# Preparing a mixture-of-experts stage inside the last attention quad, and naming tile rows on GpSimd

## What is computed

```
x2 = rmsnorm(hid, ln2_w).reshape(-1, h)          # 2048 tokens
probs = softmax(x2 @ gate_w.T)                   # 16 experts
top_w, top_i = top_k(probs, 4); top_w /= sum(top_w)
act = silu(g) * u                                # g, u = x2 @ w1[e], 176 each
routed = einsum('te,teh->th', wfull, act @ w2)   # 4 experts of each token
shared = (silu(x2 @ sg.T) * (x2 @ su.T)) @ sh_down_w.T   # 352 wide, every token
out = hid + routed + shared
```

## Time and profile before

| | us |
|---|---|
| median of three runs (lowest, highest) | 1864.67 (1861.90, 1866.82) |
| the profiled execution | 1865.75 |
| its span | 1864.0 |
| PE busy | 1721.0 (92%) |
| DVE busy | 1156.7 (62%) |
| ACT busy | 983.2 (53%) |
| POOL busy | 500.3 (27%) |

### The profile page before, as it was taken

The page is one execution under the profiler, slowest core; times in us unless marked ns, Lnnn a source line. Parts: engine busy times, 40 slices in busy tenths (PEclk is TensorE's granted clock), DMA queues, the critical chain, the costliest instruction groups (busy, mean ns, idle before and its releaser), DMA issues. The chain is left out here.

```text
span 1864.0 us, 34272 instructions
## 1 busy us (share of the span) xinstructions
PE 1721.0 (92%) x11713; PEld 1450.5 (78%) x11722; DVE 1156.7 (62%) x2562; ACT 983.2 (53%) x2535; POOL 500.3 (27%) x554
## 2 busy tenths in 40 slices
PE   7999996897699999999999999999999967879997
PEld 6666663655588888888888888888888866679985
DVE  6689883897655656656556655555555546754444
ACT  2588875586344545444555545444444433445553
POOL 4133321253311111111112111111111110257773
PEclk7799996998899999999999999999999985989999
DMA  4111121302100100100100101000000015243347
GB/s 151 59 37 36 37 81 36 110 8 94 49 13 1 46 12 12 36 12 12 35 24 23 46 1 35 13 12 24 12 12 1 1 37 148 75 127 114 125 145 235
DMA packets 48916, 97.39 MB, mean 52 GB/s; under 512 B 7467, under 2 KB 29147, under 8 KB 47765
## 3 DMA queue, kind: packets, MB, share of 16 engines
q1 hardware_dynamic: 40023, 72.44, 12.8%
q0 software_dynamic: 7584, 21.37, 3.9%
q10 hardware_dynamic: 1144, 1.40, 0.2%
HBM read 73.85 MB, written 20.97 MB: 51 GB/s over the span
## 5 line engine op out<-in xcount | busy, mean ns | idle before, releaser
L1939 POOL TENSOR_TENSOR hold_wq<-hold_wq,ca_rsum 128x512 f32<-128x512 f32 x128 | 133.4, 1043 | 826.8 <-DVE ca_rsum L2167 826.8
L1835 ACT ACTIVATE hold_wq<-hold_wq,ca_nb,ca_evens 128x128 f32<-128x128 f32 x256 | 123.4, 484 | 242.4 <-DVE ca_nb L2162 242.4
L1835 ACT ACTIVATE hold_wq<-hold_wq,ca_nb,c_rqs 128x128 f32<-128x128 f32 x256 | 123.4, 483 | 225.5 <-DVE ca_nb L2162 225.5
L712 DVE TENSOR_REDUCE a_mx<-a_s 128x2 f32<-128x512 f32 x256 | 164.8, 681 | 41.8 <-PE a_s L584 39.1
L503 ACT ACTIVATE a_prob<-a_s 128x512 f32<-128x512 f32 x256 | 146.8, 605 | 59.2 <-PE a_s L604 58.0
L1949 PE MATMUL ca_qk<-c_xTh,ca_wqkv_h 128*128 128x512 f32 x384 | 161.5, 420 | 11.3 <-DVE ca_wqkv_l L2112 11.3
L1951 PE MATMUL ca_qk<-c_xTh,ca_wqkv_l 128*128 128x512 f32 x384 | 152.3, 397 | 0.0
L1950 PE MATMUL ca_qk<-c_xTl,ca_wqkv_h 128*128 128x512 f32 x384 | 151.6, 395 | 0.0
L2064 PE MATMUL ca_acc<-ca_wo_h,ca_oT_h 128*128 128x256 f32 x512 | 145.4, 284 | 0.0
L2066 PE MATMUL ca_acc<-ca_wo_h,ca_oT_l 128*128 128x256 f32 x512 | 144.6, 282 | 0.0
L2065 PE MATMUL ca_acc<-ca_wo_l,ca_oT_h 128*128 128x256 f32 x512 | 144.5, 282 | 0.0
(11 more groups left out here) (428 smaller groups left out, 4853.3 us busy)
## 6 DMA issues: line engine op xcount, KB each, us to landing
w_all<-slot_results SPq DMA_DIRECT2D x16, 512.0 KB, 7.4
mw_raw<-in_d_expert_w SPq DMA_DIRECT2D x16, 352.0 KB, 4.3
a_heads<-a_osb SPq DMA_DIRECT2D x124, 32.0 KB
a_wraw<-a_heads SPq DMA_DIRECT2D x31, 128.0 KB, 2.1
mw_down<-in_d_expert_d SPq DMA_DIRECT2D x1, 2816.0 KB
token_rows<-mw_rows SPq DMA_DIRECT2D x1, 2176.0 KB
hold_wk<-in_c_wkT SPq DMA_DIRECT2D x1, 2064.0 KB, 8.2
hold_wq<-in_c_wqT SPq DMA_DIRECT2D x1, 2064.0 KB
```

The lines of the kernel that those rows point to most:

```text
L712: dve.tensor_reduce(mx[:, b % 2, :, h], s1_bank(b, u)[:, :, :], AX.X, ALU.max)\
L1835: ins = act.activation(prob[:, p, b, :], prob[:, p, b, :], ACT.Exp, bias=nb[:, p, b:b + 1], scale=row_scale[layer][:, r:r + 1], accum_out= ...
L1939: pool.tensor_tensor(prob[:, k % 2, :, :], prob[:, k % 2, :, :], rsum[:, k % 2, :].unsqueeze(2).broadcast_to([P, GB, TOKENS]), ALU.mult)\
```

## The change

Three things are changed, and the rest follows from them.

1. A class `EarlyExpertData` lays tiles at fixed addresses over buffers that the last attention quad no longer uses. The transposed x of the attention and that of the experts are one tile (`own_T`, `early.x`). While the second layer starts, SP loads the shared gate and value weights, the gate's, the norm's and experts 14, 15 and 6. In the last quad, by tables like those of before: DVE's statistics of groups 0 to 2 (`gauge`, behind units 7, 11, 15), POOL's roots (`root`), DVE's normalisation (`shrink`, units 9, 13 and the end), PE's turns of pairs 0 to 3 (`FLIP`, units 10, 11, 14, 15), high and low halves of the weights (ACT, POOL; units 6, 7, 8, 9, 12). The sort stage keeps group 3's rows, `raw_d`, and 13 experts.
2. `named` is made by POOL from `tile_of` itself, comparison and multiplication in one operation, 64 of 128x80, for 16 on DVE and 64 on ACT. It waits for `placed`. Finding starts three units later.
3. POOL, which waits for nothing then, makes the low halves of nine experts, six ahead of the naming, three behind it. `down` no longer has a place free from the start, and is loaded in two parts at the end of the sort stage, behind all expert loads. X_EARLY is 14 for 22, X_AHEAD 26 for 28.

```diff
@@ attend_tokens
+        GAUGE = {7: 0, 11: 1, 15: 2}
+        ROOT = {8: 0, 12: 1}
+        SHRINK = {9: 0, 13: 1}
+        FLIP = {10: 0, 11: 1, 14: 2, 15: 3}
+        HALVE = {6: 0, 7: 1}
+        PARTS = {8: 0, 9: 1, 12: 2}
...
+                sp.wait_ge(x_lo, PAIRS)
+                sp.dma_start(early.raw_gu[:, :], early.gu_w).then_inc(ld_s, 16)
+                for n in range(len(EARLY_EXPERTS)):
+                    sp.dma_start(early.raw_w[n][:, :], early.expert_w[EARLY_EXPERTS[n]]).then_inc(ld_s, 16)
...
+                        if end in FLIP:
+                            turn(PAIRS + FLIP[end], rows, min(v_count(WHOLE - 1, 0, end + 1), UNITS * WHOLE))
...
-X_EARLY, X_AHEAD, X_BUFS = 22, 28, 40
+X_EARLY, X_AHEAD, X_BUFS = 14, 26, 40
+LATER_EXPERTS = (0, 1, 2, 3, 4, 5, 7, 8, 9, 10, 11, 12, 13)
+LOWERED = 9
...
@@ sort_and_share
             def _(sp):
...
-                sp.dma_start(first.down[:, :], first.w2).then_inc(first.ld_d, 16)
                 sp.wait_ge(meta_ready, 1)
-                sp.wait_ge(xn_ready, BATCHES)
+                sp.wait_ge(xn_ready, GB)
...
-                for n in range(RAW_BUFS, EXPERTS):
+                for n in range(RAW_BUFS, len(LATER_EXPERTS)):
                     sp.wait_ge(first.w_lo, n - RAW_BUFS + 1)
                     first.load(sp, n)
+                sp.wait_ge(u_psum, UNITS_S)
+                sp.dma_start(first.down[:, 0:LAST_DOWN], first.w2[:, 0:LAST_DOWN]).then_inc(first.ld_d, 16)
+                sp.wait_ge(acc_psum, UNITS_S)
+                sp.wait_ge(hid_lo, UNITS_S)
+                sp.wait_ge(d_lo, 1)
+                sp.dma_start(first.down[:, LAST_DOWN:], first.w2[:, LAST_DOWN:]).then_inc(first.ld_d, 16)
...
+                for n in range(6):
+                    first.split_lo(pool, early, n)
+                pool.wait_ge(ld_c, 32)
+                pool.wait_ge(placed, 1)
+                for b in range(BATCHES):
+                    after(pool, found_psum, b - DEEP + 1)
+                    for k in range(TOPK):
+                        c = P + b + BATCHES * k
+                        ins = pool.tensor_scalar(named[:, b % DEEP, k, :], times, tile_of[:, b, k:k + 1], cons[:, c:c + 1],
+                                                 ALU.is_equal, ALU.mult)
+                    ins.then_inc(named_ready, 1)
+                for n in range(6, LOWERED):
+                    first.split_lo(pool, early, n)
...
-                for m in range(PAIRS + 1):
-                    if m < PAIRS:
-                        turn(m)
-                    if m >= 1:
-                        score(m - 1)
-                for t in range(UNITS_S + 2):
+                for m in range(4):
+                    score(m)
+                turn(0)
+                turn(1)
+                gates_and_values(0)
+                turn(2)
+                turn(3)
+                for m in TURNS:
+                    score(m)
+                for t in range(1, UNITS_S + 2):
...
@@ routed_experts, down(0)
-                        pe.wait_ge(first.ld_d, 16)
+                        pe.wait_ge(first.ld_d, 32)
```

More of the change, by code:

```diff
@@ L1300, with pair_of, prepare_text_free @@
 UNITS = GROUPS * 4
[L1303 removed]
+def pair_of(rows, m, n):
+    return rows[:, m // 2, n, :, 2 * P * (m % 2):2 * P * (m % 2) + 2 * P]
+def prepare_text_free(nc, work, x_sb, ident, xn, ctx_sb, own_T, image_T, rqs, nrqs, ob, g, loads, fetch):
     with ExitStack() as stack:
@@ L1613, in fetch, with attend_tokens @@
         self.load_v(sp, 0, 0)
-def attend_tokens(nc, x_sb, ident, image_parts, own_parts, first, cols, gate, work, rqs, nrqs, ln1, before):
+def attend_tokens(nc, x_sb, ident, image_T, own_T, first, cols, gate, work, rqs, nrqs, ln1, before, early):
     QC = 4 * HD
@@ L2024, in body @@
                         now = step(layer, i, k)
+                        end = final(layer, i, k)
                         turns = 0 if now is None else len([n for n in TURN if n <= now])
+                        if end is not None:
+                            turns = PAIRS + len([n for n in FLIP if n <= end])
                         g1, h1 = ((k + 1) // 4) % 4, (k + 1) % 4
@@ L2793, in _ @@
+                hidden(0)
+                rest_x(2)
+                rest_x(3)
+                rest_hid(0)
                 dve.wait_ge(l_psum, 1)
@@ L2819, in _ @@
                    .then_inc(meta_ready, 1)
+                hidden(2)
+                rest_hid(1)
                 dve.wait_ge(n_psum, 1)
@@ L3153, in _, with expert_layer @@
                            .then_inc(added, 1)
-def expert_layer(nc, res, ln2, gate_w, gu_w, down_w, expert_w, expert_d, consts, slots, results, filled, gate, before, out):
+def expert_layer(nc, res, early, down_w, expert_w, expert_d, consts, slots, results, filled, gate, before, out):
     x_sb, ident = res["x"], res["ident"]
@@ L3160, in expert_layer @@
         m = Scope(nc, middle, "w")
-        big = m.sb("all", [P, EXPERTS * 2 * W_COLS], F32R)
+        m.sb("all", [P, EXPERTS * 2 * W_COLS], F32R)
         first = ExpertWeights(nc, middle, expert_w, expert_d)
-        sort_and_share(nc, x_sb, ident, first, big, ln2, gate_w, gu_w, down_w, consts, gate, slots, filled)
-        routed_experts(nc, x_sb, ident, first, big, before, slots, results, out)
+        sort_and_share(nc, x_sb, ident, first, early, down_w, consts, gate, slots, filled)
+        routed_experts(nc, x_sb, ident, first, early.big, before, slots, results, out)
 def gated_layers(nc, io, out):
```

532 lines of the change are left out of this document (297 added, 235 removed).

## The result

The changed kernel is slower by half a per cent: 1874.24 us median (1870.26 to 1883.37), the kernel before 1864.45, ratio 1.0054, 95% interval 1.0031 to 1.0077. Forecast were 1847.5 and a range of 1829 to 1864. The profiled execution took 1870.89 us, its span 1869.1. Two other sets of runs gave 1.0062 (1.0027 to 1.0096) and 1.0065 (1.0037 to 1.0094).

A forecast was written before the change was run, and what follows sets the result against it. The sort stage, with PE not full and DVE and ACT near full, was taken as the bound ahead of 1612 us. Terms 2.5 - 30.1 + 8 + 2.5 = -17.1 gave 1848.6 profiled, 1847.5 median, range 1829 to 1864.

The forecast's parts named there:

- (a): Last attention quad: turns, statistics and splits put into it lengthen PE's part by 2.5 us, range 1.5 to 4.5.
- (b): Sort stage, counted from its first statistics (S): ends at S+92.7 instead of 122.8 us, -30.1 us.
- the low bound: Sort stage, end of score products with full clock behind the first four pairs: 15.8 us from S.
- the sixth split: Sort stage: GpSimd's sixth low-half split, behind a late expert load, holds naming until S+41.8, 5.5 us behind the places.
- I take their middle, 0.40: 64 x 0.40 = 25.6: Sort stage, naming on GpSimd: 64 operations at 0.40 us, between two nearest rows' estimates, take 25.6 us.
- The upper bound, 0.50: Naming on GpSimd: highest estimated time of one 128x80 operation, 0.50 us, from the bf16 row's 3.3 ns per column.
- R1: Slower rival: GpSimd's comparison is dear, 0.85 us per naming operation, +28.8 us, 1876; sign turns at 0.67; chance 0.12.
- Behind the naming: End of sort stage: remaining PE products and DVE's last addition and splits take 25.0 us after the last batch is found.
- (c): Start of routed stage: PE's first y product waits 4 to 12 us on the later-issued down weights, taken as +8.
- (d): Routed stage: changed gather counts leave GpSimd two operations more, at 1.25 us each, +2.5 us.
- R3: Given-back rival: naming as forecast, down load up to 20 us late, GpSimd can't make it up; 12 more, 1859.5; chance 0.14.

The follow-up runs named there:

- f1: The changed kernel itself, run again on one chip beside f2, f3 and f4: 1880.9 us, ratio 1.0062 to the kernel before.
- f2: Changed kernel with naming by 64 DVE operations, 8 early gathers for 14, 20 ahead for 26, more down weights loaded early: 1857.4 us, ratio 0.9952 to the kernel before.
- e1: Changed kernel with naming given back to DVE and ACT: 1897.9 us, ratio 0.9999 to the kernel before.
- f4: Same kernel as e1 (changed kernel, naming back on DVE and ACT), on a second chip: 1863.2 us, ratio 0.9979 to the kernel before.
- f3: Changed kernel with the same 64 naming operations issued by DVE instead of GpSimd: 1864.9 us, ratio 0.9987 to the kernel before.
- e4: Kernel before the change with 64 trial operations of eight forms on idle GpSimd, results unused: 1897.9 us in its single execution.

## Why the prediction was wrong

By its steps, on the first set's trace:

- **(a) attention**, +2.5: 0.4. In the later sets the stage's start lay between -1.0 and +4.7 us of 1529.11, so no more is known than that it is small.
- **(b) sort stage, ahead of the naming**. The scores were forecast at S+20.5 and ended at S+17.1, nearer the low bound. The 32 products of ready rows began at S, 0.213 us apart; the granted clock rose from half to full during unit 0's gates (their spacing falls from 0.43 to 0.23 us at 1539.6), and the later score products were 0.11 apart. The places were forecast at S+36.3 and came at S+36.3, but that is luck: the scores were 3.4 us early, and the chain from the logits took 19.2 us where some 16 were allowed, with DVE steps held beside GpSimd's subtractions (above). Naming was forecast from S+41.8 and began at S+38.1, held by the sixth split as foreseen. This part is worth 3.7 us more than forecast.
- **The step that failed** is "I take their middle, 0.40: 64 x 0.40 = 25.6". It measured 47.9, +22.3. An operation alone is 0.63 (40.3 us), 14.7 of the miss; the other 7.6 are operations stretched beside DVE, of which the sum had no term. The slope of 3.3 ns a column was the bf16 row's and right; the fixed part, 0.237 from an operation with constants, lacked the two per-partition scalars and the comparison. The rows that were near in shape had neither a comparison nor two per-partition scalars, and I read the difference of the two as one of output type, where their operations differ too. That the slope is the same may be chance. The upper bound, 0.50, should not have been a bound: no row showed a comparison on GpSimd, and R1 said so. R1, with a chance of 0.12, was right that the comparison is dear, but its 7.7 ns a column is not: it is 3.3 and a fixed part of 0.36 us. Its price of 0.85 and break-even of 0.67 have the measured 0.75 between them. The Trainium skill (GPSIMD Engine Reference, 3.1, Elementwise) has "use DVE for elementwise" as the rule, and the runs agree: DVE does the operation at 0.25 us and GpSimd at 0.63. Its 12 cycles an element for data-dependent branching, an estimated 10 ns at the 1.2 GHz of the same section, do not describe this comparison, which takes 3.3 ns a column.
- **Behind the naming**, 25.0: 31.2. Missing from the sum was what GpSimd does to DVE: 3.9 us on the indices, for which the addition, and by it PE (4.75 us), waited. The remaining 1.5 us are not traced; the granted clock was 0.86 there.
- **(c) and (d)**, 8 + 2.5: 9.8. The sum is right by luck, since its terms were off in opposite ways. The wait on the down load was 4.3 us, in the range of 4 to 12. The other 5.4 us are more than twice (d), which counted two operations more in the routed stage; eight more gathers are there, six ahead of the first scatter and two between. f1 had no wait at its first y and was still 5.9 us longer than the kernel before, from PE's first turn on. How much of it is GpSimd's and how much the clock (0.92 for 0.99 in the last 72 to 77 us) was not tested.
- **Not in the sum at all**: the drain. I costed the late load where it is used and not at the barrier that it crosses; where it goes wrong PE starts some 18 us later behind the stage's work, and the profiled execution is 12.9 us longer than that of the first set. Two of that set's six executions are in the upper group.

25.6 to 47.9 and 25.0 to 31.2 make 28.5 us, the gains on (a) and on naming's start 5.8: 1848.6 + 28.5 - 5.8 - 0.7 (c, d) = 1870.6, measured 1870.9. R3 was right in one half: GpSimd can't make up what is put behind the stage, and f2's routed part gives back 16 us. Its other half, a down load that comes too late, is not what f2 shows, since its first y had no wait. Even with naming as cheap as before, the change would not have given what was forecast: e1 and f4 gain 0 to 4 us.

## What to carry to other kernels

Before work is moved to an idle engine, price it on that engine with its very operands: comparison and per-partition scalars, not only shape and type. And look at what the engine that it leaves does meanwhile: here each held the other up. At the end of a block, ask what each engine's drain waits for: GpSimd's waited for its gathers to land, and they took up to 16 us beside a large load, so let the small transfers land first. Ask of each saving what is the next bound, here the gathers and scatters of one queue.

## What the runs showed of the hardware that I had not expected

- A GpSimd operation and a DVE operation that run beside each other can stretch one another: GpSimd's 0.63 us up to 2.13, DVE's 0.20 to 2.63, the DVE one ending with GpSimd's.
- GpSimd's tensor_scalar on 128x80: 0.26 us with constants, 0.41 with two per-partition scalars, 0.63 with two such scalars and a comparison; DVE does the latter at 0.25 apiece (four in 1.01, f3).
- GpSimd's drain at the end of the block lasted from 4.3 to 20.6 us, and ended 0.6 to 1.0 us behind the last landing of its gathers in the five traces that have it (before, after, f1, f3, f4). SP's took 0.2 us with a 2332 KB load under way.
- A gather landed 2.7 us behind its issue at best, and 15 to 17 us behind it beside that load (f1, f3, f4).
- Between chips, the kernel before differs by up to 1.8% (medians of 1864.5 and 1898.1 us). Its trace and that of e4, nearly the same kernel on a slower chip, differ by 32.1 us, of which 31.3 lie behind the sort stage. Why is open.
